# Second attention: the pattern of every second k replica added by a third matmul, evicted by ScalarE

## The chip, the cores and the metric

The kernel runs on one core of one Trainium2 chip, as one program in one launch. The core's engines are TensorE (PE), VectorE (DVE), ScalarE (ACT) and GpSimd (POOL), each with its own instruction queue, worked off in order; SyncE (SP) issues most of the transfers. The engines meet through semaphores. The metric is the device time of one execution in microseconds (us), lower is better.

## What is computed

The reference is a chain of four layers on 2048 tokens of width 128 (eight sequences of 256). Each layer is a mixer and a feed-forward part. The change touches the mixer of the third layer (in the kernel: the second attention, `l == 2`), an attention of 16 heads of width 8 with a relative position bias that depends on the distance only and is constant beyond the near keys:

```python
x = layernorm(h)
q, k, v = split_heads(x @ Wq), split_heads(x @ Wk), split_heads(x @ Wv)   # 8 x 16 heads x 256 x 8
scores = q @ k^T + bias[bucket(distance), head]
h = h + gate(softmax(scores) @ v @ Wo)
```

The second layer has an attention too (`l == 1`, without the bias). Both are made by the same functions.

## The kernel before, in words

Activations lie transposed in SBUF: 128 channels on the partitions, 2048 tokens along the free side, in four chunks (c = 0 to 3) of 512. A head has 8 channels, too few for a matmul's contraction, so each head gets a strip of 32 partitions, of which the last 24 hold three copies of its 8 channels (as high and low fp16 parts) and the first 8 helper rows. The helper rows of k serve to add constants to the scores: a row of ones (it meets the negated row maximum) and four rows that are 1 for far keys (they meet the far bias). This constant part of k is the tile `k_pat`, 128 partitions x 512, fp16. For the second attention GpSimd zeroes it (L1033) and twelve small transfers from `far_keys` put its rows in (`key_rows`, L2363 and L2366); the semaphore `k_rows` counts them. It stands at 64 after the first attention and at 256 (`16 * HH * 4`) once those of the second have landed.

Ahead of the main loop comes a preparation. A string, `PREPARE[l]`, writes down its units, and every engine goes through the same string and does its own part of each unit:
- D (D0 to D7): the dense product of a chunk with Wq or Wk on PE (L652). ACT makes the high fp16 part with the bias (`high`, L820), DVE the remainder (`low`, L937).
- R (R0 to R31): a replica. n even is q, n odd is k; four groups of heads for each of four chunks. PE adds up two matmuls, high part and low part, in a PSUM bank (L700, L701), and one engine evicts the bank to `q_st` or `k_st`. The q replicas are plain copies on ACT (L853). In the second attention DVE evicts all k replicas and adds `k_pat` in the same instruction (L981). In the first attention every second k replica is evicted by ACT with a per-partition bias, which works there since the pattern is the same for all keys. `by_act(l, m)` says who evicts, `evicted(A, m)` turns that into a semaphore and a count to wait for.
- WO, V: the output weights and the v projection, each with a bank of its own. R, WO and V share a ring of four banks: a unit waits until the one four places before it is evicted.
- F (F0 to F7): the first batch's scores (four L642 matmuls) into the one early pair of banks, and their row maxima on DVE (`row_maxima`: four custom instructions at L960). Each F on PE waits for the maxima of the F before it.
- X, N on ACT: fp16 copies of the normalised input (L832) and of the near bias table (L838), read by GpSimd later. B on DVE: the far bias rows and the conversion of the next layer's integer weights.

The main loop starts with S1.0 (again L642, for the next batch). It waits on PE for the last three evictions and for the maxima of F7. Each of its passes works on one batch: scores, row maxima on DVE, exponentials on ACT (L876), probabilities times v on PE (L806).

Nothing but the string and the semaphores sets the order. The wait for the rows stands once, on DVE, ahead of the whole preparation (L966).

Of the kernel before, what the change touches and what calls it, by code (L numbers as in the profile page):

```python
# [16 lines left out]
P = 128  # L17
# [17 lines left out]
HH = 4  # L35
# [52 lines left out]
def build(nc, x_in, pack0, packc, pack1, pack1f, pack2, far_keys, spread, onehot, wint, pack3, ew1, ew2, out):  # L88
    C0, N0 = columns(PACK0)
    with ExitStack() as ctx:  # L90
# [34 lines left out]
        ps = ctx.enter_context(nc.psum_tensor("ps", [P, 8, CH], F32))  # L125
# [357 lines left out]
        k_pat = take(CH // 2).bitcast(F16)  # L483
        rep_sel = take(4 * CH // 2).bitcast(F16).rearrange("p (x n) -> p x n", x=4)
        halves = [take(CH // 2).bitcast(F16) for _ in range(8)]
        hi_f, lo_f = halves[0:4], halves[4:8]
# [19 lines left out]
        ident16 = sb("ident16", [P, P], F16)  # L506
# [91 lines left out]
            return n if n < 4 else n % 2  # L598

        def by_act(l, m):  # L600
            return m % 2 == 0 or (l == 1 and m // 2 % 2 == 1)

        def evicted(A, m):
            l = 1 if A is ASEMS[0] else 2
# [17 lines left out]
        k_rows = sem("k_rows")  # L622
# [8 lines left out]
        def attn_pe(pe, l, A):  # L631
# [33 lines left out]
            for kind, n in PREPARE[l]:  # L665
                if kind in ("LG", "R", "WO", "V"):
                    bank = BANKS[l][(kind, n)]
                    r = IN_BANK[l].index((kind, n))
                    if r >= 4:
                        wait_bank(r - 4)  # L670
                if kind == "D":
                    dense(n)
                    if l == 2 and n == 3:
                        pe.wait_ge(rows_ready, 1)
                elif kind == "LG":
                    for t in range(4 * n, 4 * n + 4):
                        mm = pe.matmul(ps[:, bank, t % 4 * EXPERTS:(t % 4 + 1) * EXPERTS], xn[:, t * P:(t + 1) * P], WF("gate_w"),
                                       start=True, stop=True)
                    mm.then_inc(MOE["lg_ps"], 1)
                elif kind == "V":  # L680
                    for t in range(4 * n, 4 * n + 4):
                        mm = pe.matmul(ps[:, bank, (t % 4) * P:(t % 4 + 1) * P], xn[:, t * P:(t + 1) * P], WA(w, "Wv"),
                                       start=True, stop=True)
                    mm.then_inc(A["v_ps"], 1)
                elif kind == "WO":
                    pe.wait_ge(sel_done, 2)
                    pe.wait_ge(*A.at("v_zeroed", SEL_MADE))
                    for j in range(2):
                        pe.matmul(ps[:, bank, j * P:(j + 1) * P], ident, WA(w, "Wo")[:, 2 * j * P:(2 * j + 1) * P], start=True, stop=False)
                        pe.matmul(ps[:, bank, j * P:(j + 1) * P], shift16, WA(w, "Wo")[:, (2 * j + 1) * P:(2 * j + 2) * P], start=False, stop=True)  # L690
                    pe.matmul(ps[:, bank, 2 * P:2 * P + STRIP], shift16, WC("sel_sum"), start=True, stop=True).then_inc(A["wo_ps"], 1)
                elif kind == "R":
                    c, g, k = n // (2 * G4), n % (2 * G4) // 2, n % 2
                    d = 2 * c + k
                    if g == 0:
                        pe.wait_ge(*A.at("proj_lo", d + 1))
                    if n == 0:
                        pe.wait_ge(sel_done, 2)
                        pe.wait_ge(*A.at("v_zeroed", SEL_MADE))
                    pe.matmul(ps[:, bank, :], rep_sel[:, 2 * k, g * P:(g + 1) * P], hi_f[d % 4], start=True, stop=False)  # L700
                    pe.matmul(ps[:, bank, :], rep_sel[:, 2 * k + 1, g * P:(g + 1) * P], lo_f[d % 4], start=False, stop=True)\  # L701
                        .then_inc(A["rep_ps"], 1)
                elif kind == "F":
                    if n == 0:
                        pe.wait_ge(*A.at("proj_lo", 4))
                        for m in (2 * G4 - 3, 2 * G4 - 2, 2 * G4 - 1):
                            pe.wait_ge(*evicted(A, m))
                    else:
                        pe.wait_ge(*released(A, "S1", n - 1, -1))
                    scores(FIRST, n, -1)  # L710
# [101 lines left out]
        def attn_act(act, l, A):  # L812
# [11 lines left out]
            for kind, n in PREPARE[l]:  # L824
                if kind == "D":
                    high(n)
                    if l == 1 and n == 3:
                        act.wait_ge(k_rows, 16 * HH)
                        act.activation(k_ones, k_pat[:, 0:1], ACT.Copy).then_inc(A["rep_act"], 1)
                elif kind == "X":  # L830
                    xn_wait(act, 2)
                    act.activation(x16[:, n, 0, :], chunk(xn, n), ACT.Copy).then_inc(rows_ready, 1)  # L832
                elif kind == "N":
                    if n == 0:
                        act.wait_ge(tabs_in, 32)
                        act.wait_ge(S3["zeroed"], 16 * 7)
                    heads = slice(n * HEADS // 2, (n + 1) * HEADS // 2)
                    act.activation(near16[:, heads, :], near32[:, heads, ::-1], ACT.Copy).then_inc(near_high, 1)  # L838
                elif kind == "WO":
                    bank = BANKS[l][(kind, n)]  # L840
                    act.wait_ge(*A.at("wo_ps", 1))
                    act.activation(wo2.rearrange("p j n -> p (j n)"), ps[:, bank, 0:2 * P], ACT.Copy).then_inc(A["wo_done"], 1)
                    act.activation(by_group(sel_den)[:, :, 1, :], by_group(ps[:, bank, 2 * P:2 * P + STRIP])[:, :, 1, :], ACT.Copy).then_inc(A["wo_done"], 1)
                    act.activation(by_group(sel_den)[:, :, 0, :], by_group(WC("sel_sum"))[:, :, 0, :], ACT.Copy).then_inc(A["wo_done"], 1)
                elif kind == "R" and by_act(l, n):
                    c, g, k = n // (2 * G4), n % (2 * G4) // 2, n % 2
                    act.wait_ge(*A.at("rep_ps", n + 1))
                    to = (k_st if k else q_st)[:, g, c * CH:(c + 1) * CH]
                    if k:
                        act.wait_ge(*A.at("rep_act", 1))  # L850
                        act.activation(to, ps[:, BANKS[l][("R", n)], :], ACT.Identity, bias=k_ones).then_inc(A["rep_act"], 1)
                    else:
                        act.activation(to, ps[:, BANKS[l][("R", n)], :], ACT.Copy).then_inc(A["rep_act"], 1)  # L853
# [63 lines left out]
        def attn_dve(dve, l, A):  # L917
# [44 lines left out]
                                                       row_max[1 - par][:, qb, g, h:h + 1])  # L962
                        ins.then_inc(A["ttr"], 1)

            dve.wait_ge(k_rows, 16 * HH * (1 if l == 1 else 4))
            for kind, n in PREPARE[l]:  # L966
                if kind == "D":
                    low(n)
                elif kind == "LG":
                    dve.wait_ge(*MOE.at("lg_ps", n + 1))  # L970
                    dve.wait_ge(S3["zeroed"], 16 * 7)
                    dve.tensor_copy(rt["lg"][:, 4 * n:4 * n + 4, :],
                                    ps[:, BANKS[l][(kind, n)], 0:4 * EXPERTS].rearrange("p (t e) -> p t e", t=4)).then_inc(MOE["lg_sb"], 1)
                elif kind == "V":
                    dve.wait_ge(*A.at("v_ps", n + 1))
                    dve.tensor_tensor(v_sb[:, 4 * n:4 * n + 4, :].rearrange("p t c -> p (t c)"), ps[:, BANKS[l][(kind, n)], :], WA(w, "bv"),
                                      ALU.add).then_inc(A["v_done"], 1)
                elif kind == "R" and not by_act(l, n):
                    c, g = n // (2 * G4), n % (2 * G4) // 2
                    dve.wait_ge(*A.at("rep_ps", n + 1))  # L980
                    dve.tensor_tensor(k_st[:, g, c * CH:(c + 1) * CH], ps[:, BANKS[l][(kind, n)], :], k_pat, ALU.add).then_inc(A["rep_dve"], 1)  # L981
                elif kind == "F":
                    if l == 2 and n == 0:
                        dve.wait_ge(rows_out, 32)
                    row_maxima(n, -1)
                elif kind == "T":
                    if n < 3:
                        route1_choose(dve, n)
                    else:
                        route1_near(dve)  # L990
                elif kind == "B":
                    far_rows()
                    dve.wait_ge(w2_in, 16)
                    ups = 2 * HID2 * P
                    dve.tensor_scalar(w2f[:, ups:], wint_sb[:, ups:], 1.0 / (127.0 * W_DQ), None, ALU.mult)
                    dve.tensor_scalar(w2f[:, 0:ups], wint_sb[:, 0:ups], W_DQ / 127.0, None, ALU.mult).then_inc(w2_ready, 1)
# [1579 lines left out]
```

## Time and profile before

| | before |
|---|---|
| median of 3 runs | 835.33 us (833.63 to 836.16) |
| the profiled execution's own time | 835.67 us |
| its span | 833.9 us |
| PE busy | 702.1 us, 84% |
| DVE busy | 643.3 us, 77% |
| ACT busy | 507.6 us, 61% |
| GpSimd busy | 388.3 us, 47% |

The profiled execution took 1.8 us more than its span, the distance from the first to the last instruction in the trace. All points in time below count from the start of the span. The preparation of the second attention lies at 332 to 372 us, its main loop at 372 to about 500 us. The shares are means over the whole program; what a stage is worth has to be read in that stage.

### The profile page before, as it was taken

Reading aid. Unit: us, or ns where it says so; the run is one execution under the profiler, and the core shown is the slowest. Engines: PE = TensorE matmul, PEld = TensorE weight load, DVE = VectorE, ACT = ScalarE, POOL = GpSimd, SP = SyncE. Lnnn points to the kernel's source line nnn. Section 1 sums busy time; section 2 is a strip of 40 time slices with the busy share of each in tenths; the row PEclk is TensorE's granted clock in tenths of the full one; section 3 lists DMA queues with packets and bytes.
Section 4 is the critical chain, followed back from the end, with each engine's and each line's share of the span. In section 5 each row is a group of like instructions: output and inputs, shape, how many; then the busy total and the mean of one; then the engine's idle time right before and its main releaser. Section 6 shows DMA issues by size and latency. Waiting matters only on the chain.

```text
span 833.9 us, 13257 instructions
## 1 busy us (share of the span) xinstructions
PE 702.1 (84%) x4706; PEld 352.3 (42%) x4720; DVE 643.3 (77%) x1290; ACT 507.6 (61%) x746; POOL 388.3 (47%) x385
## 2 busy tenths in 40 slices
PE   5996987989979977869999989994877888888986
PEld 2332453444446753334444444441323344444453
DVE  3988777888727745787989924489899999899995
ACT  4788645888865545626666653668454555555473
POOL 0000305686836652041000002028999999999962
PEclk9996997999999996987999999997999999999999
DMA  8600000000144119100000000305447444645441
GB/s 348 277 1 0 4 1 1 1 31 23 37 117 132 44 28 298 42 0 2 3 2 3 2 2 1 126 16 166 159 154 276 147 149 143 201 162 178 156 161 51
DMA packets 30433, 75.97 MB, mean 91 GB/s; under 512 B 4335, under 2 KB 14008, under 8 KB 29344
## 3 DMA queue, kind: packets, MB, share of 16 engines
q1 hardware_dynamic: 26048, 67.41, 23.7%
q0 software_dynamic: 4320, 7.72, 2.7%
q8 instruction: 38, 0.62, 0.3%
q14 instruction: 27, 0.22, 0.1%
HBM read 59.28 MB, written 17.01 MB: 91 GB/s over the span
## 4 chain that ended last, share of the span: by engine, by line
PE 34%; DVE 22%; issue 18%; POOL 13%; ACT 10%; DMA 3%; SPq 0%; DVEq 0%; POOLq 0%; ACTq 0%
POOL arena L2231 7%; PE ps L806 4%; DVE ttr_out L960 4%; DVE xq L960 4%; DVE arena L2156 3%; DVE band L2163 3%; POOL exp_in L2198 3%; PE ps L784 2%; PE ps L642 2%; PE ps L295 2%; PE ps L1448 2%; ACT arena L876 2%; PE ps L652 1%; PE ps L772 1%; PE ps L1215 1%
## 5 line engine op out<-in xcount | busy, mean ns | idle before, releaser
L2156 DVE TENSOR_TENSOR_SCAN arena<-ps,arena 128x1024 f32<-128x1024 f32 x64 | 146.6, 2291 | 18.5 <-ACT ps L2032 9.8
L876 ACT ACTIVATE arena<-ps 128x1024 f32<-128x1024 f32 x128 | 124.8, 1025 | 35.3 <-PE ps L795 25.8
L2032 ACT ACTIVATE ps<-arena,negA 128x1024 f32<-128x1024 f32 x64 | 71.5, 1118 | 102.0 <-DVE arena L2156 101.7
L1866 PE MATMUL ps<-band,w 128*128 128x512 f32 x256 | 120.1, 592 | 0.0
L2163 DVE TENSOR_TENSOR band<-arena,ps 128x1024 f32<-128x1024 f32 x64 | 76.6, 1196 | 2.3 <-PE ps L1751 2.3
L2231 POOL TENSOR_TENSOR arena<-arena,gate 128x1024 f32<-128x1024 f32 x32 | 75.6, 2366 | 4.3 <-DMA gate<-b_dram 3.4
L2231 POOL TENSOR_TENSOR arena<-arena 128x1024 f32<-128x1024 f32 x32 | 75.2, 2364 | 0.3
L806 PE MATMUL ps<-arena 128*32 128x256 f32 x1024 | 70.9, 397 | 1.0 <-ACT arena L876 1.0
L1751 PE MATMUL ps<-xq,sel 128*128 128x512 bf16 x115 | 35.7, 383 | 41.8 <-DVE band L2163 39.1
L1074 POOL COPY arena<-arena 128x128 f32<-128x128 f32 x32 | 8.4, 296 | 123.7 <-PE ps L806 107.2
L1866 PEld LDWEIGHTS ps<-band,w 128*128 128x128 f32 x256 | 48.6, 190 | 40.2 <-issue 30.6
L784 PE MATMUL ps<-arena 32*128 32x256 f16 x512 | 49.9, 280 | 12.8 <-ACT arena L876 3.8
L2198 POOL DMA_INDIRECT exp_in<-wf,wa x32 | 32.2, 1007 | 57.3 <-DVE wa L2121 49.8
L642 PE MATMUL ps<-arena 32*128 32x256 f16 x512 | 50.2, 281 | 8.8 <-DVE arena L960 4.5
L1550 POOL DMA_INDIRECT e_out<-arena,band x39 | 37.9, 971 | 35.7 <-ACT arena L1499 21.7
L960 DVE CUSTOM_DVE_ANT_0 xq<-ps,wf 128x256 bf16<-128x256 f32 x128 | 46.5, 420 | 7.2 <-issue 7.2
L960 DVE CUSTOM_DVE_ANT_0 ttr_out<-ps,wf 128x256 bf16<-128x256 f32 x128 | 46.6, 420 | 6.8 <-issue 6.1
L947 DVE TENSOR_REDUCE xq<-ps 128x4 f16<-128x1024 f32 x32 | 38.4, 1222 | 11.1 <-PE ps L642 10.6
L947 DVE TENSOR_REDUCE arena<-ps 128x4 f16<-128x1024 f32 x32 | 38.7, 1220 | 7.1 <-PE ps L642 6.5
L1751 PEld LDWEIGHTS ps<-xq,sel 128*128 128x128 bf16 x128 | 8.0, 97 | 73.9 <-DVE band L2163 67.7
L806 PEld LDWEIGHTS ps<-arena 128*32 128x32 f32 x1024 | 27.4, 111 | 27.0 <-issue 12.5
L1381 POOL DMA_INDIRECT e_in<-arena,band x32 | 32.0, 1001 | 10.2 <-issue 8.5
(404 smaller groups left out, 1620.4 us busy)
## 6 DMA issues: line engine op xcount, KB each, us to landing
gate<-b_dram SPq DMA_DIRECT2D x32, 512.0 KB, 3.7
arena<-b_dram SPq DMA_DIRECT2D x32, 512.0 KB, 4.4
wf<-pack1f_dram SPq DMA_DIRECT2D x1, 3076.0 KB, 15.2
wf<-bias_rows SPq DMA_DIRECT2D x1, 3072.0 KB, 15.4
exp_in<-band SPq DMA_DIRECT2D x2, 1032.0 KB, 5.0
exp_out<-band SPq DMA_DIRECT2D x2, 1024.0 KB, 17.9
e_in<-band SPq DMA_DIRECT2D x2, 1024.0 KB, 21.7
arena<-e_out SPq DMA_DIRECT2D x4, 512.0 KB, 5.7
```

Of the source, the lines that this page charges most:

```text
L642: mm = pe.matmul(to[:, a:a + SEQ], q_st[h, g, (b + 1) * SEQ + qb * P:(b + 1) * SEQ + (qb + 1) * P], k_st[h, g, (b + 1) * SEQ:(b + 2) * SEQ ...
L784: mm = pe.matmul(out_[:, a:a + SEQ], k_st[h, g, b * SEQ + kb * P:b * SEQ + (kb + 1) * P], q_b[par][h, g, :], start=(l == 1 or kb == 0), st ...
L806: mm = pe.matmul(ps[32 * h:32 * h + 32, 6, (i // 2) * SEQ:(i // 2 + 1) * SEQ], v_b[pp][:, kb, i * HH + h, :], probs[i % 2][:, h, kb, :], s ...
L876: act.activation(probs[g % 2][:, 2 * pr:2 * pr + 2, :, :].rearrange("p h k n -> p (h k n)"), PAIRS[l][("S2", i, b)], ACT.Exp).then_inc(A[" ...
L947: dve.tensor_reduce(firsts.rearrange("p b h -> p h b"), scores.rearrange("p (h b n) -> p h b n", h=2, b=2), AX_X, ALU.max, negate=True).th ...
L960: ins = dve.tensor_tensor_reduce(ttr_outs[unit % 2][:, n, :], scores[:, n * SEQ:(n + 1) * SEQ], bias_q[:, g * HH + h, WIN - a - SEQ:WIN - ...
L1866: mm = pe.matmul(ps[:, j, :], ident, hc[i % 2][:, j * CH:(j + 1) * CH], start=False, stop=True, skip_group_check=True)
L2032: act.activation(dA_ps, dt3[:, cb, hf * HALF:(hf + 1) * HALF], ACT.Exp, scale=negA[:, cb * STATE + n:cb * STATE + n + 1]).then_inc(M["dA"], 1)
L2156: dve.tensor_tensor_scan(hst[i % 2], dA_ps, dbu[i % 4], 0.0, ALU.mult, ALU.add).then_inc(M["scan"], 1)
L2163: dve.tensor_tensor(hc[i % 2], hst[i % 2], pair(3), ALU.mult).then_inc(M["hc"], 1)
L2198: pool.indirect_dma_start(out=exp_in[k], out_offset=bass.IndirectOffsetOnAxis(ap=idx_s[:, k, t:t + 1], axis=0), in_=x_nat[:, t, :], in_off ...
L2231: pool.tensor_tensor(dbu[i % 4], du[:, cb, hf * HALF:(hf + 1) * HALF], b_sb[i % 4], ALU.mult).then_inc(M["dbu"], 1)
```

## The change

In the second attention, the k replicas n = 3, 7, 11, ..., 31 (eight of sixteen) get their pattern from a third matmul (`ident16` times `k_pat`) into the same bank, and ACT evicts them by a plain copy. The wait for all the rows moves from the head of DVE's preparation to the two places where the pattern is read: DVE's remaining eight additions, and the third matmuls on PE. What is left at the head asks for 64, which is there since the first attention. No function is new.

```diff
--- before.py
+++ after.py
@@ -598,7 +598,7 @@
             return n if n < 4 else n % 2
 
         def by_act(l, m):
-            return m % 2 == 0 or (l == 1 and m // 2 % 2 == 1)
+            return m % 2 == 0 or m // 2 % 2 == 1
 
         def evicted(A, m):
             l = 1 if A is ASEMS[0] else 2
@@ -698,8 +698,12 @@
                         pe.wait_ge(sel_done, 2)
                         pe.wait_ge(*A.at("v_zeroed", SEL_MADE))
                     pe.matmul(ps[:, bank, :], rep_sel[:, 2 * k, g * P:(g + 1) * P], hi_f[d % 4], start=True, stop=False)
-                    pe.matmul(ps[:, bank, :], rep_sel[:, 2 * k + 1, g * P:(g + 1) * P], lo_f[d % 4], start=False, stop=True)\
-                        .then_inc(A["rep_ps"], 1)
+                    patterned = l == 2 and k and by_act(l, n)
+                    mm = pe.matmul(ps[:, bank, :], rep_sel[:, 2 * k + 1, g * P:(g + 1) * P], lo_f[d % 4], start=False, stop=not patterned)
+                    if patterned:
+                        pe.wait_ge(k_rows, 16 * HH * 4)
+                        mm = pe.matmul(ps[:, bank, :], ident16[:, :], k_pat, start=False, stop=True)
+                    mm.then_inc(A["rep_ps"], 1)
                 elif kind == "F":
                     if n == 0:
                         pe.wait_ge(*A.at("proj_lo", 4))
@@ -846,7 +850,7 @@
                     c, g, k = n // (2 * G4), n % (2 * G4) // 2, n % 2
                     act.wait_ge(*A.at("rep_ps", n + 1))
                     to = (k_st if k else q_st)[:, g, c * CH:(c + 1) * CH]
-                    if k:
+                    if k and l == 1:
                         act.wait_ge(*A.at("rep_act", 1))
                         act.activation(to, ps[:, BANKS[l][("R", n)], :], ACT.Identity, bias=k_ones).then_inc(A["rep_act"], 1)
                     else:
@@ -962,7 +966,7 @@
                                                        row_max[1 - par][:, qb, g, h:h + 1])
                         ins.then_inc(A["ttr"], 1)
 
-            dve.wait_ge(k_rows, 16 * HH * (1 if l == 1 else 4))
+            dve.wait_ge(k_rows, 16 * HH)
             for kind, n in PREPARE[l]:
                 if kind == "D":
                     low(n)
@@ -978,6 +982,7 @@
                 elif kind == "R" and not by_act(l, n):
                     c, g = n // (2 * G4), n % (2 * G4) // 2
                     dve.wait_ge(*A.at("rep_ps", n + 1))
+                    dve.wait_ge(k_rows, 16 * HH * (1 if l == 1 else 4))
                     dve.tensor_tensor(k_st[:, g, c * CH:(c + 1) * CH], ps[:, BANKS[l][(kind, n)], :], k_pat, ALU.add).then_inc(A["rep_dve"], 1)
                 elif kind == "F":
                     if l == 2 and n == 0:
```

On DVE, at the head of the second attention's preparation, before (L242 ends the normalising, L937 are the low parts of D0 to D3, L981 the k evictions, `rep_ps` counts replicas on PE):

```order
L937 SCALAR_TENSOR_TENSOR arena<-ps,bq_s,arena 128x512 [waits attn_proj_hi,k_rows]
L937 SCALAR_TENSOR_TENSOR arena<-ps,wa,arena 128x512 [waits attn_proj_hi]
L937 SCALAR_TENSOR_TENSOR arena<-ps,bq_s,arena 128x512 [waits attn_proj_hi]
L937 SCALAR_TENSOR_TENSOR arena<-ps,wa,arena 128x512 [waits attn_proj_hi]
L981 TENSOR_TENSOR arena<-ps,arena 128x512 [waits attn_rep_ps] x6
L955 MEMSET wait_here 1x1 [waits attn_s1_ps,rows_out]
```

and now (L937 has become L941, L981 has become L986):

```order
L941 SCALAR_TENSOR_TENSOR arena<-ps,bq_s,arena 128x512 [waits attn_proj_hi,k_rows]
L941 SCALAR_TENSOR_TENSOR arena<-ps,wa,arena 128x512 [waits attn_proj_hi]
L941 SCALAR_TENSOR_TENSOR arena<-ps,bq_s,arena 128x512 [waits attn_proj_hi]
L941 SCALAR_TENSOR_TENSOR arena<-ps,wa,arena 128x512 [waits attn_proj_hi]
L986 TENSOR_TENSOR arena<-ps,arena 128x512 [waits k_rows,attn_rep_ps] x3
L959 MEMSET wait_here 1x1 [waits attn_s1_ps,rows_out]
```

Of the six k evictions between the low parts and F0, three are left, and each waits for the rows. (The first low part still names `k_rows`, with the count that is met.)

On DVE, at the end of the preparation, before (from the weight conversion of unit B on: R27, F6, R29, V3, F7, R31, and L1020 of the main loop; an F is one L955 and four pairs of L960):

```order
L996 TENSOR_SCALAR wint<-wint 128x768
L981 TENSOR_TENSOR arena<-ps,arena 128x512 [waits attn_rep_ps]
L955 MEMSET wait_here 1x1 [waits attn_ttr,attn_s1_ps]
L960 ISA ttr_out,arena<-ps,wf 128x256
...
L960 ISA arena 128x1
L981 TENSOR_TENSOR arena<-ps,arena 128x512 [waits attn_rep_ps]
L976 TENSOR_TENSOR arena<-ps,wa 128x512 [waits attn_v_ps]
L955 MEMSET wait_here 1x1 [waits attn_ttr,attn_s1_ps]
L960 ISA xq,arena<-ps,wf 128x256
...
L960 ISA arena 128x1
L981 TENSOR_TENSOR arena<-ps,arena 128x512 [waits attn_rep_ps]
L1020 TENSOR_SCALAR arena<-arena 128x32 [waits attn_ttr]
```

and now:

```order
L1001 TENSOR_SCALAR wint<-wint 128x768
L959 MEMSET wait_here 1x1 [waits attn_ttr,attn_s1_ps]
L964 ISA ttr_out,arena<-ps,wf 128x256
...
L964 ISA arena 128x1
L986 TENSOR_TENSOR arena<-ps,arena 128x512 [waits k_rows,attn_rep_ps]
L980 TENSOR_TENSOR arena<-ps,wa 128x512 [waits attn_v_ps]
L959 MEMSET wait_here 1x1 [waits attn_ttr,attn_s1_ps]
L964 ISA xq,arena<-ps,wf 128x256
...
L964 ISA arena 128x1
L1025 TENSOR_SCALAR arena<-arena 128x32 [waits attn_ttr]
```

R27 ahead of F6 and R31 behind F7 are gone.

On PE, from the dense products on, now (before, the row L705 isn't there, and L702 was L701; R0 to R3, then R4):

```order
L652 MATMUL ps<-xn,wa 128x512 [waits xn_ready,attn_bq_done]
L652 MATMUL ps<-xn,wa 128x512 [waits xn_ready] x3
L700 MATMUL ps<-arena 128x512 [waits sel_done,attn_v_zeroed,attn_proj_lo,rows_ready]
L702 MATMUL ps<-arena 128x512
L700 MATMUL ps<-arena 128x512 [waits attn_proj_lo]
L702 MATMUL ps<-arena 128x512
L700 MATMUL ps<-arena 128x512
L702 MATMUL ps<-arena 128x512
L700 MATMUL ps<-arena 128x512
L702 MATMUL ps<-arena 128x512
L705 MATMUL ps<-arena,ident 128x512 [waits k_rows]
L700 MATMUL ps<-arena 128x512 [waits attn_rep_act]
L702 MATMUL ps<-arena 128x512
```

The third matmul stands behind the two of R3, with a wait for the rows of its own.

## Rows read from the trace of the kernel before

**Rows 1.** Busy time by stretch: stretch, its length, busy us (instructions) by engine, clock, DMA.

```profile
345.00:360.00 15.00, 12.67 (x69) 6.07 (x66) 14.66 (x58) 10.19 (x17) 4.32 (x2) 1.00 0.01 1
```

**Rows 2.** Groups of instructions between 338 and 373 us: busy us, mean ns | idle before.

```profile
L853 ACT ACTIVATE arena<-ps 128x512 f16<-128x512 f32 x16 | 9.5, 596 | 14.9 <-PE ps L701 14.8
```

**Rows 3.** Who waited for whom, 338 to 373 us: us in total, times, longest.

```profile
ACT arena L853 <- PE ps L701: 14.8, 12, 4.7
...
DVE arena L937 <- DMA arena<-far_keys_dram: 2.9, 1, 2.9
```

**Rows 4.** Timeline of 332 to 341 us: start, length, engine, line [idle before <- releaser].

```profile
332.11 3.60 PE L652 MATMUL ps<-xn,wa 128*128 128x512 f32 x8
...
333.69 0.69 DVE L242 TENSOR_TENSOR xn<-arena,ps 128x512 f32<-128x512 f32 x1 [0.64 <-ACT arena L261]
...
335.74 0.69 ACT L820 ACTIVATE arena<-ps,wa 128x512 f16<-128x512 f32 x1 [0.17 <-PE ps L652]
337.28 0.75 DVE L937 SCALAR_TENSOR_TENSOR arena<-ps,bq_s,arena 128x512 f16<-128x512 f32 x1 [2.90 <-DMA arena<-far_keys_dram]
...
338.13 0.38 PE L700 MATMUL ps<-arena 128*128 128x512 f16 x1 [2.43 <-issue]
...
338.35 0.38 PE L701 MATMUL ps<-arena 128*128 128x512 f16 x1
...
339.92 1.28 DVE L981 TENSOR_TENSOR arena<-ps,arena 128x512 f16<-128x512 f32 x2
```

**Rows 5.** Timeline of 95.5 to 98 us, the same place in the first attention.

```profile
96.27 0.75 DVE L937 SCALAR_TENSOR_TENSOR arena<-ps,bq_s,arena 128x512 f16<-128x512 f32 x1
...
97.47 0.38 PE L700 MATMUL ps<-arena 128*128 128x512 f16 x1
```

**Rows 6.** Timeline of PE, 344 to 369 us: units F0, F2, F3, F4 and F7.

```profile
344.82 0.39 PE L642 MATMUL ps<-arena 32*128 32x256 f16 x4
...
350.85 0.39 PE L642 MATMUL ps<-arena 32*128 32x256 f16 x4 [0.77 <-DVE arena L960]
...
353.44 0.39 PE L642 MATMUL ps<-arena 32*128 32x256 f16 x4 [0.36 <-DVE arena L960]
...
356.02 0.39 PE L642 MATMUL ps<-arena 32*128 32x256 f16 x4 [0.34 <-DVE arena L960]
...
368.82 0.39 PE L642 MATMUL ps<-arena 32*128 32x256 f16 x4 [3.02 <-DVE arena L960]
```

**Rows 7.** Timeline of 366 to 373 us: R27, F6, R29 and R31 on DVE, S1.0 on PE.

```profile
366.69 0.69 DVE L981 TENSOR_TENSOR arena<-ps,arena 128x512 f16<-128x512 f32 x1
367.30 0.43 DVE L960 CUSTOM_DVE_ANT_0 ttr_out<-ps,wf 128x256 bf16<-128x256 f32 x1
...
368.68 0.69 DVE L981 TENSOR_TENSOR arena<-ps,arena 128x512 f16<-128x512 f32 x1
...
371.26 0.69 DVE L981 TENSOR_TENSOR arena<-ps,arena 128x512 f16<-128x512 f32 x1
...
372.17 0.61 PE L642 MATMUL ps<-arena 32*128 32x256 f16 x4 [1.98 <-DVE arena L981]
```

**Rows 8.** Busy time by stretch where the clock changes (columns as in rows 1).

```profile
131.50:132.00 0.50, 0.24 (x1) 0.27 (x2) 0.43 (x2) 0.50 (x3) 0.00 (x0) 0.75 0.00 0
370.50:371.00 0.50, 0.00 (x0) 0.00 (x0) 0.50 (x5) 0.00 (x0) 0.00 (x0) 0.69 0.00 0
384.00:384.50 0.50, 0.50 (x7) 0.13 (x4) 0.50 (x5) 0.26 (x1) 0.00 (x0) 0.66 0.00 0
```

**Rows 9.** Timeline of PE at the end of the first attention's preparation.

```profile
129.18 0.39 PE L642 MATMUL ps<-arena 32*128 32x256 f16 x4 [1.21 <-DVE arena L947]
...
131.76 0.55 PE L732 MATMUL ps<-band,w 128*128 128x129 f32 x1 [1.22 <-ACT arena L851]
```

**Rows 10.** Busy time by stretch: the main loop's start, and one later pass.

```profile
372.00:382.00 10.00, 9.18 (x78) 4.20 (x82) 5.87 (x37) 5.12 (x5) 0.00 (x0) 0.50 0.01 2
405.60:420.60 15.00, 14.73 (x207) 7.28 (x206) 13.56 (x78) 9.80 (x11) 0.53 (x2) 1.00 0.01 3
```

## The prediction

> **What bounds the kernel now.** I read the views in this order. First the busy time by stretch [rows 1]: between 345 and 360 us, inside the preparation of the second attention, DVE is busy 14.66 of 15 us and PE 12.67, while ACT has 10.19. DVE is the engine with no room here, PE comes next, ACT is third. Then the groups of that stage [rows 2]: ACT evicts its 16 q replicas at 596 ns each, while DVE's 16 k evictions take 0.69 us each [rows 7]. Then who waited for whom [rows 3]: ACT waited 14.8 us for PE in the same stage, and DVE waited once, 2.9 us, for the row transfers from far_keys. So the reader is to see two things: one long wait at the head of the stage, and a DVE queue which is late from there to the end.
>
> The head, in order of time [rows 4]: the last normalised chunk leaves DVE at 334.38, with the first high parts (L820) already made by ACT, and PE is done with the four dense products at 335.71 (332.11 + 3.60). But the first low part (L937) starts at 337.28, when the row transfers have landed, and the first replica matmul (R0) at 338.13, a hole of 2.43 us on PE. The low part doesn't read the pattern; it only stands behind the wait. In the first attention, where the transfers were there, the low part started at 96.27 and R0 at 97.47, 1.20 us later [rows 5].
>
> The rest: each F unit on PE (four L642 matmuls into the one early pair) waits for the row maxima of the F before it on DVE. The brackets on PE before F2, F3, F4 and F7 say 0.77, 0.36, 0.34 and 3.02 us [rows 6]. The stage ends when the first main-loop unit S1.0 starts, at 372.17, after 1.98 us of waiting for the last k eviction (R31), which DVE began at 371.26 [rows 7].
>
> **The change part by part.** I walk the queues from the head to S1.0 and write how far each point moves.
>
> *Rows awaited where needed.* low(0) can start when hi(0) is done and DVE is free of the normalising, about 334.4; R0 would be possible 1.20 us later, at 335.6, but PE itself is busy until 335.71. R0 moves from 338.13 to 335.75, by -2.4. The new waits: DVE waits for the rows at its first k eviction (R1), PE at the third matmul of R3. DVE comes to R1 after low(3), which needs ACT's hi(3) (335.74 + 0.69 = 336.43) and ends at about 337.2, so the landing at 337.28 costs DVE some 0.1 us. PE starts R3 at 335.75 + 3 x 0.44 = 337.1 and its third matmul at 337.5, after the landing. Behind PE's wait stand R4 and everything else of PE, and ACT's evictions behind those, but if the rows came later, the old order would be late by the same amount plus R0 to R3. The other row waits (DVE 8 evictions, PE 8 third matmuls) are always met; I take them at nothing.
>
> *The third matmul.* Successive f16 matmuls of 512 columns start 0.22 us apart, 338.13 and 338.35 [rows 4]. Eight are added: 1.8 us of PE. Bounds: nothing where PE waits for DVE anyway, 1.8 us where it is the bound.
>
> *The eviction.* Eight DVE evictions go. Each holds the next one up by 0.61 us, 366.69 to 367.30 [rows 7], together 4.9 us. ACT gets eight plain copies of 0.6 us, 4.8 us, against the 14.8 us in which it waits for PE in this stage [rows 3]. Bounds of the DVE gain: 4.9 if DVE set every piece, 0 if PE set all of them.
>
> Point by point:
> - R0 to F0 took 6.69 (338.13 to 344.82) [rows 4, 6]. PE sets it. Three third matmuls (R3, R7, R11) add 0.66. In return PE no longer meets the DVE backlog: before, DVE was in its low parts until 339.92, 1.8 us after R0, and each bank had to wait for it [rows 4]. Twelve pairs at 0.44 and the Wo unit of about 1.0 make 6.3, so 0.4 were such holes. Net +0.2: F0 moves by -2.2.
> - F0 to F2: the chain is dense product, high part, low part, F1 on DVE. R13 stays on DVE, R15 goes, but F2 only waits for F1. No gain: -2.2.
> - F2 to F3 took 2.59: on DVE F2 (1.38, as from 367.30 to 368.68 [rows 7]) and two evictions. Now R19 is gone and PE becomes the bound: 0.32 for F2, four pairs (1.75), one third matmul (0.22) = 2.29. Gain 0.3: -2.5.
> - F3 to F4 took 2.58, with 0.34 of waiting on PE [rows 6] plus the tail of the unit before, since the next matmul could start some 0.1 us before the modelled end. F3 now starts on DVE without a backlog, so this goes: -2.9.
> - F4 to F5: PE sends R22, R23, two dense products, and waits for their high and low parts. Same length: -2.9. F5 to F6: PE-bound, one third matmul: -2.7, but what counts next is DVE.
> - F6 to F7: DVE has F5, the V addition, the far rows and weight conversions, R27, F6; it is bound by itself, and R27 goes (0.61): F7 moves by -2.9 - 0.6 = -3.5.
> - F7 to S1.0: R31 goes from DVE, and S1.0 now waits for the maxima of F7, 0.6 earlier: **-4.1 at S1.0**.
>
> After S1.0 the order is the same, and nothing there waits on an absolute time: the rows, bias tables and conversions are ahead of it, and GpSimd's chain for S2.0 (from ACT's copies of xn) gets its input about 1.7 us earlier, as ACT's queue runs ahead. The whole shift of 4.1 us should reach the end. Against the profiled execution's own time of 835.67 this gives 831.6; the median of the runs shown is 0.34 lower, so 831.2.
>
> **The clock.** The granted clock fell from 1.00 to 0.50 at about 370.7, after a hole of 3.02, 1.4 us of matmuls, and the next hole; it came back at about 384.2 [rows 8]. In that time the first pass runs at 1.2 GHz with PE busy 9.18 of 10 us and DVE 5.87, where a later pass has DVE 13.56 of 15 [rows 10]. My walk leaves holes of 2.2 (before F7) and 1.2 us (before S1.0) with 1.5 us of matmuls between. In the first attention the holes were 1.21 and 1.22 us [rows 9], and the granted clock fell all the same, within the half us from 131.5 [rows 8]. So I keep the loss in the forecast.
>
> The Trainium skill, page "TensorE: Matmul & The Clock Gate", section "Why this matters for your kernels", says that it is long idle gaps between bursts of matmuls that bring the halved clock, and short ones don't. By that rule this change, which shortens the longest gap, could keep the full rate, and the time would be that of rival 1. The first attention's rows speak against it: the clock fell there after gaps of 1.2 us.
>
> **The rivals.**
> 1. *The clock stays up at the start of the main loop.* For it: the long hole shrinks from 3.02 to 2.2 us, and the hole of 2.43 us at the head did no harm. Against: the first attention. Price: from 372.2 to 384.2 PE runs at half rate, busy 0.92, which at most gives back 5.5 us; DVE idles 0.41 of it against 0.10 in a later pass, 3.7 us. I take 4: 827.2.
> 2. *Only the wait counts; the eviction gives nothing.* PE is 84% busy in the middle of the stage [rows 1], and the third matmuls take on PE what DVE gains. Then only -2.2 is left: 833.0.
> 3. *The change does nothing:* the row wait merely moves to R1 and R3 and PE is held by full banks behind R1 (ring of four) instead. For it: the landing time doesn't move. Against: R1 to R4 can be made meanwhile, and the low parts (2.6 us) are then done. 835.3.
> 4. *Slower: the clock stays down longer.* The half rate would have to reach into the second pass, where PE is busy 14.73 of 15 us [rows 10] and loses nearly half of each us. More than 4.1 + 2.5 us of loss needs over 13 us at half rate beyond the 12 of now; with half a pass more than that (20 us, 10 us of loss) the time is 841. For it: in the first attention the clock came and went twice. Against: in this one it came back and stayed.
>
> **How the numbers follow.** Forecast (around 4 us, 3 to 5.5) 0.53, rival 1 0.17, rival 2 0.16, rival 3 0.08, rival 4 0.06. No change can be told within 0.3%, 2.5 us. Faster: the forecast but for its edge, 0.50, rival 1, and a third of rival 2, since 2.2 is near 2.5: 0.72. Same: 0.03 + 0.11 + 0.08 = 0.22. Slower: 0.06. The range goes down to rival 1 and up past rival 2: 827.2 to 834.2.
>
> **What the profile after would show.** R0 at 335.7 with no wait for far_keys ahead of the low parts; F0 near 342.6, F4 near 353.1, F7 near 365.3, S1.0 near 368.1 and released by L960's successor, not by a k eviction; ACT with 24 replica copies in the stage and never the one that PE waits for; the clock at 0.50 from about 367. I would be wrong if a third matmul costs more than 0.22 us beside a weight load, if ACT's copies of xn and of the near tables delay an eviction on which a bank hangs, or if the clock does otherwise.

## The result, and the profile after

The changed kernel takes 832.46 us (median of 20 runs, 829.72 to 834.71) against 835.50 us for the kernel before (20 runs, 833.63 to 840.60). The ratio is 0.9959, 95% interval 0.9950 to 0.9969: 3 us faster, inside the forecast range, 1.3 us above the forecast time. Not all of it comes from the changed stage: 1.1 us arise at the very end of the program, as shown below. The profiled execution took 833.18 us with a span of 831.4.

Points in time of two executions are best compared from one mark just ahead of the stage, because the stages before it differ by up to 2.3 us from execution to execution (in one by 6 to 8). I take the start of the last L242, the last chunk of the normalised input on DVE: 333.69 us before, 334.63 after. From here on "at 35.42" means so many us behind this mark. The last column is ACT's first copy of the main loop, L863 in the kernel before and L867 in the changed one; it comes once per pass.

| us behind the mark | R0 | F0 | F2 | F4 | F7 | S1.0 | first L863/L867 |
|---|---|---|---|---|---|---|---|
| before | 4.44 | 11.13 | 17.16 | 22.33 | 35.13 | 38.48 | 40.94 |
| after | 1.86 | 8.81 | 14.84 | 19.40 | 32.57 | 35.42 | 37.89 |
| moved by | -2.58 | -2.32 | -2.32 | -2.93 | -2.56 | -3.06 | -3.05 |
| forecast | -2.4 | -2.2 | -2.2 | -2.9 | -3.5 | -4.1 | |

The head of the stage, timeline of the changed kernel on DVE and PE, answering to [rows 4]:

```profile
334.63 0.69 DVE L242 TENSOR_TENSOR xn<-arena,ps 128x512 f32<-128x512 f32 x1 [0.64 <-ACT arena L261]
335.28 0.75 DVE L941 SCALAR_TENSOR_TENSOR arena<-ps,bq_s,arena 128x512 f16<-128x512 f32 x1
...
336.49 0.38 PE L700 MATMUL ps<-arena 128*128 128x512 f16 x1
```

The low part follows the normalising without a pause, R0 comes 1.21 us later (1.20 in the first attention), and the wait for far_keys is gone from the row. The F units F3, F4 and F7 and the main loop's S1.0 on PE, answering to [rows 6] and [rows 7]:

```profile
351.84 0.39 PE L642 MATMUL ps<-arena 32*128 32x256 f16 x4
...
354.03 0.39 PE L642 MATMUL ps<-arena 32*128 32x256 f16 x4
...
367.20 0.39 PE L642 MATMUL ps<-arena 32*128 32x256 f16 x4 [2.96 <-DVE arena L964]
...
370.05 0.61 PE L642 MATMUL ps<-arena 32*128 32x256 f16 x4 [1.27 <-ACT arena L857]
```

The brackets of F3 and F4 have vanished: PE sets that part now. But the hole before F7 is 2.96 us, where it was 3.02. What DVE does in it is unit B, and its first row is not the one of before (DVE and POOL, timeline of the changed kernel):

```profile
362.20 1.04 DVE L926 COPY b_far<-wf 128x16 f32<-128x16 f32 x1
```

```profile
358.98 4.23 POOL L1067 TENSOR_TENSOR band<-arena,band 64x1024 f16<-64x1024 f32 x2
```

A copy of 128x16 elements takes 1.04 us and ends at 363.24, just as GpSimd's correction of the near table ends (363.21). In the kernel before the same copy started at 363.98, when GpSimd was nearly done (at 364.22), and took 0.28 us:

```profile
362.09 2.13 POOL L1062 TENSOR_TENSOR band<-arena,band 64x1024 f16<-64x1024 f32 x1
...
363.98 0.28 DVE L922 COPY b_far<-wf 128x16 f32<-128x16 f32 x1
```

By the busy time of the same 345 to 360 us [rows 1], which holds somewhat later work now, DVE went from 14.66 to 12.52 of 15 us and PE from 12.67 to 13.38.

The bracket before S1.0 names ACT's last eviction (L857), of R31. In this execution it ended at 369.42 and the maxima of F7 at 369.73, so that the maxima came last, as forecast. In the second execution (below) the clock fell while PE made R30 and R31: there the eviction ended at 369.76 and the maxima at 369.51, and PE did wait for ACT.

At the end of the program SyncE waits for the last transfer to `out_dram` (who waited for whom, the kernel before, then the kernel with the eviction alone):

```profile
SPq L90 <- DMA out_dram<-xT: 2.9, 1, 2.9
```

```profile
SPq L90 <- DMA out_dram<-xT: 1.8, 1, 1.8
```

From the end of DVE's last instruction to the landing of this transfer it takes 3.22 and 3.21 us in the two profiled executions of the kernel before, and 2.11 to 2.13 us in all twelve profiled executions of the other kernels, those of the changed one included. So 1.1 us of what each of them gains in time has nothing to do with S1.0. Why the transfer lands sooner stays open: no run changes it alone.

### The profile page after: what moved, and what is told of

Its sections match the earlier page's. It is cut to its first block, busy times and chain, and to the rows that moved or that the text cites. A ratio compares the mean times of both kernels' runs of the same rounds, so it can differ in the third digit from the quotient of the medians.

```text
span 831.4 us, 13289 instructions
## 1 busy us (share of the span) xinstructions
PE 705.7 (85%) x4714; PEld 354.2 (43%) x4728; DVE 639.7 (77%) x1282; ACT 511.7 (62%) x754; POOL 387.8 (47%) x385
## 4 chain that ended last, share of the span: by engine, by line
PE 36%; DVE 22%; issue 15%; POOL 12%; ACT 10%; DMA 3%; SPq 0%; DVEq 0%; POOLq 0%; ACTq 0%
POOL arena L2236 8%; PE ps L810 4%; DVE ttr_out L964 4%; DVE xq L964 4%; DVE arena L2161 3%; DVE band L2168 3%; PE ps L788 2%; PE ps L295 2%; PE ps L642 2%; PE ps L1453 2%; ACT arena L880 1%; PE ps L776 1%; PE ps L652 1%; POOL exp_in L2203 1%; PE ps L1220 1%
## 5 line engine op out<-in xcount | busy, mean ns | idle before, releaser
L857 ACT ACTIVATE arena<-ps 128x512 f16<-128x512 f32 x40 | 23.4, 595 | 23.2 <-PE ps L702 22.7
```

## The experiments

All but two were timed side by side with the kernel before (one was only profiled, one gave no result). "x" is the ratio to the kernel before with its 95% interval. The runs of one kernel spread by mostly 3 to 5 us, those of the kernel before by up to 9, so that the intervals are 0.002 to 0.0035 to each side. The profile, read from the mark, carries most of the verdicts. Each is one execution, though. Most pieces repeat to 0.1 us, but two things differ between executions of the same kernel: how late the rows land (it moves F0 by up to 0.6 us) and when the clock falls (it moves S1.0 by up to 0.6 us).

| | R0 | F0 | F7 | S1.0 | first L863/L867 | x |
|---|---|---|---|---|---|---|
| before, again | 4.63 | 11.32 | 35.34 | 38.68 | 41.15 | |
| wait only | 1.85 | 8.93 | 32.96 | 36.30 | 38.76 | 0.9941 (0.9920 to 0.9961) |
| eviction only | 4.05 | 11.20 | 34.97 | 38.66 | 41.12 | 0.9982 (0.9962 to 1.0002) |
| changed, again | 1.85 | 8.81 | 32.57 | 35.55 | 38.02 | 0.9939 (0.9913 to 0.9966) |
| changed, third | 1.85 | 9.06 | 32.81 | 36.29 | 38.76 | 0.9943 (0.9924 to 0.9962) |
| one matmul more | 1.85 | 9.46 | 33.44 | 37.05 | 39.51 | 0.9950 (0.9933 to 0.9966) |
| holes filled | 1.85 | 8.93 | 32.70 | 35.54 | 36.96 | 0.9940 (0.9920 to 0.9960) |
| GpSimd behind the far rows | 1.85 | 8.99 | 33.70 | 37.39 | 39.86 | 0.9962 (0.9942 to 0.9981) |
| GpSimd behind all of B | 1.85 | 8.81 | 31.55 | 34.40 | 36.86 | 0.9946 (0.9926 to 0.9966) |
| B ahead of F0 | 1.85 | 8.81 | 29.54 | 32.17 | 33.58 | 0.9900 (0.9865 to 0.9935) |
| wait only, B ahead of F0 | 1.86 | 8.34 | 31.61 | 34.95 | 37.42 | 0.9935 (0.9907 to 0.9963) |

**The wait alone.** The kernel before, with

```diff
-            dve.wait_ge(k_rows, 16 * HH * (1 if l == 1 else 4))
+            dve.wait_ge(k_rows, 16 * HH)
...
                     dve.wait_ge(*A.at("rep_ps", n + 1))
+                    dve.wait_ge(k_rows, 16 * HH * (1 if l == 1 else 4))
```

> The wait for the rows moved to where the pattern is read, every k replica still evicted by DVE. If the gain of the change is made of two parts that add (wait 2.3 to 2.6 us, eviction 0.5 to 1.6 us): S1.0 starts 2.4 to 2.6 us earlier after the last normalised chunk than before (35.9 us instead of 38.5), and the time is about 2.4 us under the kernel before (ratio 0.9971). If only the eviction counts and the wait is given back behind R1: no earlier S1.0, ratio 1.000.

S1.0 at 36.30, 2.18 us earlier than before; the time is 0.0059 down, 5 us by that interval's middle, where 2.4 was expected. The interval's upper end, 0.9961, is 3.3 us. Its own timeline on DVE and PE shows what is left of the wait:

```profile
336.81 2.08 DVE L982 TENSOR_TENSOR arena<-ps,arena 128x512 f16<-128x512 f32 x3 [0.50 <-DMA arena<-far_keys_dram]
...
337.55 0.39 PE L700 MATMUL ps<-arena 128*128 128x512 f16 x1 [0.60 <-DVE arena L982]
```

Half a us at R1, and PE feels it: R5 shares R1's bank and waits 0.60 us for its eviction. In the second execution of the same kernel the rows had landed before DVE came to R1; there F0 stands at 8.34 instead of 8.93, and S1.0 at 35.72 instead of 36.30. So the wait alone brings S1.0 2.2 to 2.8 us ahead of the first execution before, by how late the rows land.

**The eviction alone.** The changed kernel with the wait for all rows back at the head of DVE.

> The eight evictions moved to ACT with the third matmul, the wait for all rows left at the head of DVE. If the parts add: R0 as before, F0 0.4 us later than before (three more matmuls on PE), S1.0 about 1.3 us earlier by the walk, less 0.8 us if DVE's first copy of unit B meets GpSimd's long operation as it does in the changed kernel; ratio 0.9985 to 0.9995. If the eviction gives nothing: ratio 1.000 or, by 1.8 us of matmuls, 1.002.

From R0 to F7 it takes 30.92 us, before 30.69: nothing gained, where 0.5 us was expected at S1.0 with the longer copy in unit B. The copy took 1.05 us here too. That S1.0 is no earlier than before has to do with the clock, which fell here ahead of F7, so that the matmuls between F7 and S1.0 ran at half rate. The ratio allows anything from no gain to 3 us, and the 1.1 us of the last transfer are in it.

**Both again, side by side.**

> The changed kernel once more, on the same chip and in the same rounds as the wait alone with B moved. Ratio to the kernel before 0.995 to 0.997. The first pass of the main loop took 17.61 us with the clock back 13.2 us after the first L867, where the kernel before and the wait alone took 16.4 with the clock back after 8.4 to 9.7 us. If that belongs to the change: 17.6 us again. If it is chance from one execution to the next: either of the two.

> The wait alone, in the same rounds and on the same chip as the whole change. S1.0 again 36.3 us after the last normalised chunk. If the eviction's 0.8 us at S1.0 reach the end, this is 0.8 us above the changed kernel, ratio higher by 0.001; if the eviction costs later what it gains before S1.0, the two are equal or this one is faster.

> The whole change, in the same rounds as the wait alone. S1.0 again 35.4 to 35.6 us after the last normalised chunk, DVE's first copy of unit B again 1.04 us. Ratio 0.001 under the wait alone, if its 0.8 us reach the end.

Side by side the wait alone has 0.9939 (0.9920 to 0.9958) and the whole change 0.9943 (0.9924 to 0.9962): they can't be told apart. (The profiled execution of the second wait-only kernel had its mark 6 to 8 us later than the others; its F7 stands at 32.35, its first L863 at 38.18.) The second timing of the whole change, 0.9939, came out below the expected 0.995 to 0.997. Both expected places of S1.0 were missed. The wait alone has it at 35.72, not 36.3, since the rows came early. The third changed execution has it at 36.29, not 35.4 to 35.6: DVE waited 0.19 us for the rows (F0 at 9.06), and the clock fell 0.3 us behind F7, so that ACT's eviction of R31 was done 0.75 us behind F7's maxima. At the first L863/L867, where the eviction should have shown 1.6 us, the mean of two wait-only executions is 38.47 and of three changed ones 38.22. Where the rows came early and the clock fell late, S1.0 is at 35.72 with the wait alone and at 35.42 with the whole change. The wait carries the gain; the eviction adds some tenths of a us.

**One look at the kernel before.**

> The kernel before, profiled once more. S1.0 again 38.0 to 38.7 us after the last normalised chunk. The first pass again 16.5 us if its length belongs to the kernel, 16.5 or 17.6 if it is chance.

S1.0 stands at 38.68, as expected. The first pass took 17.61 us here. With the changed kernel's it makes a clear picture (ACT, timeline, the first two L867 of the changed kernel, first execution, then second):

```profile
372.52 1.02 ACT L867 ACTIVATE arena<-ps 128x1024 f16<-128x1024 f32 x1 [3.10 <-PE ps L754]
...
390.13 1.03 ACT L867 ACTIVATE arena<-ps 128x1024 f16<-128x1024 f32 x1 [1.63 <-PE ps L754]
```

```profile
372.43 1.02 ACT L867 ACTIVATE arena<-ps 128x1024 f16<-128x1024 f32 x1 [2.67 <-PE ps L754]
...
388.89 1.02 ACT L867 ACTIVATE arena<-ps 128x1024 f16<-128x1024 f32 x1 [1.75 <-PE ps L754]
```

17.61 and 16.46 us for the same kernel, as 16.47 and 17.61 for the kernel before and 16.40 and 17.62 for the wait alone. In the short ones the granted clock is back at 1.00 some 8 to 10 us after the first L867, in the long ones after 13 to 14 (in the changed kernel, 384 to 388 us, 0.78 in the first execution and 1.00 in the second). So the 1.14 us by which the first pass was longer in the first trace after are chance, not the change.

**One matmul more on PE.**

> The changed kernel with a fourth matmul in each of the eight patterned replicas: the high part is sent twice, the second one overwriting the first, so that the result is the same. It doubles what the third matmuls cost on PE. If my walk is right that PE sets R0 to F0 (three of the eight), F2 to F3 (one), and that F4 to F6 (two more) is PE-bound too, as the changed kernel's trace says: F0 0.65 us later, F7 and S1.0 1.1 to 1.4 us later than in the changed kernel (36.6 to 37.0 us after the last normalised chunk), time up by as much, ratio to the kernel before about 0.996. If DVE hides the matmuls: S1.0 within 0.3 us of 35.5, ratio 0.994 to 0.995.

In this form, with the group of the added matmul left open, the kernel gave no result. With a group of its own for the added matmul it ran:

```diff
+                    if l == 2 and k and by_act(l, n):
+                        pe.matmul(ps[:, bank, :], rep_sel[:, 2 * k, g * P:(g + 1) * P], hi_f[d % 4], start=True, stop=True)
                     pe.matmul(ps[:, bank, :], rep_sel[:, 2 * k, g * P:(g + 1) * P], hi_f[d % 4], start=True, stop=False)
```

> The changed kernel with a fourth matmul in each of the eight patterned replicas: the high part is sent twice, each a group of its own, the second overwriting the first, so that the result is the same. It doubles what the third matmuls cost on PE. If PE sets R0 to F0 (three of the eight), F2 to F3 (one) and F4 to F6 (two more): F0 0.65 us later, F7 and S1.0 1.1 to 1.4 us later than in the changed kernel (36.6 to 37.0 us after the last normalised chunk), ratio to the kernel before about 0.996. If DVE hides the matmuls: S1.0 within 0.3 us of 35.5, ratio 0.994 to 0.995.

F0 at 9.46 (+0.65), as expected, F7 at 33.44 (+0.87), where 1.1 to 1.4 was expected. Units F5 and F6 of this kernel (PE, timeline):

```profile
359.92 0.39 PE L642 MATMUL ps<-arena 32*128 32x256 f16 x4
...
362.62 0.39 PE L642 MATMUL ps<-arena 32*128 32x256 f16 x4
```

F4 to F5 takes 5.69 us, with the third matmul alone 5.47, without it 5.26; F5 to F6 2.70, 2.49, 2.27. So each added matmul lies on the path there with its full 0.21 us, and F5 is 1.08 us later than in the changed kernel, F6 1.29. F7 hangs on DVE, which comes from F5 and so reached unit B late enough to be held up 0.21 us less (the copy took 0.83 us): 1.08 - 0.21 = 0.87. S1.0 (37.05) isn't read: the clock fell 0.7 us behind F7.

**GpSimd's operation and unit B.** In the changed kernel, ahead of GpSimd's correction of the near table:

```diff
                 pool.wait_ge(*A.at("v_zeroed", ALL_ZEROED + 2))
+                pool.wait_ge(band_ready, 1)
```

> The changed kernel with one wait more: GpSimd begins its correction of the near table (4.2 us) only when DVE is done with the far rows of unit B. In the changed kernel DVE's first copy of B took 1.04 us instead of 0.28 and ended when GpSimd's operation did. If the copy was held up by GpSimd's operation: it takes 0.28 us again, F7 and S1.0 start 0.76 us earlier after the last normalised chunk (34.7 instead of 35.4), and S2.0 isn't delayed, since GpSimd ends at about 369.5. If the 1.04 us have another cause: no change in the copy. The time moves by 0.8 us at most, ratio to the kernel before 0.995 to 0.996.

The copy was short again, but the time was lost two instructions later (DVE, then POOL, of this kernel):

```profile
361.78 0.17 DVE L926 COPY b_far<-wf 128x16 f32<-128x16 f32 x1
...
363.78 2.51 DVE L1001 TENSOR_SCALAR wint<-wint 128x768 f32<-128x768 int32 x1
```

```profile
363.75 4.53 POOL L1068 TENSOR_TENSOR band<-arena,band 64x1024 f16<-64x1024 f32 x2 [5.25 <-issue]
```

S1.0 came 2 us late, not 0.8 early: 1.1 of them were lost at F7, the rest behind it, where the clock had fallen already. The wait had only moved the meeting onto the weight conversion. GpSimd lost too, 4.53 us where it took 4.23 before. With `w2_ready` in place of `band_ready`, which is set when B is all done:

> The changed kernel, GpSimd's correction of the near table now behind both the far rows and the weight conversions of unit B. Where it waited for the far rows alone, the copy took 0.17 us but the second conversion 2.51 instead of 0.56. If DVE's copies and conversions are held up whenever GpSimd's operation runs: the copy takes 0.17 to 0.28 us and the conversion 0.56, unit B takes 2.5 to 2.7 us instead of 3.5, F7 and S1.0 come 0.8 to 1.0 us earlier than in the changed kernel (34.5 to 34.7 us after the last normalised chunk). S2.0 may wait: GpSimd ends at about 369.5, S2.0 stands at 373 in the changed kernel, so it shouldn't. Ratio 0.993 to 0.996. If the long operations are slow for another reason, B takes 3.5 us again.

```profile
361.25 0.17 DVE L926 COPY b_far<-wf 128x16 f32<-128x16 f32 x1
...
363.23 0.56 DVE L1001 TENSOR_SCALAR wint<-wint 128x768 f32<-128x768 int32 x1
```

F7 at 31.55, S1.0 at 34.40, both 1.02 us earlier than in the changed kernel's first execution. Most of it is the copy, 0.17 instead of 1.04 us. In time it can't be told from the change (0.9946 and 0.9943, side by side).

**Unit B elsewhere.** The changed kernel with B moved in the string from behind V2 to ahead of F0 (and its wait for `rows_out` with it).

> The changed kernel with unit B (far bias rows and weight conversion, 3.5 us on DVE there) moved from between V2 and F6 to ahead of F0, where DVE idles 3.8 us. If DVE's work between F5 and F6 is what opens the 2.96 us hole on PE and eats the gain: the hole shrinks under 0.5 us, S1.0 starts 3 to 3.7 us earlier than in the changed kernel (31.7 to 32.4 us after the last normalised chunk instead of 35.4), ratio to the kernel before about 0.992. If moreover the clock stays at 1.00 because the hole is gone: ratio 0.988 to 0.989. If PE sets the end anyway: under 1 us, ratio 0.995.

F7 at 29.54 with no bracket, S1.0 at 32.17, 3.25 us earlier than in the changed kernel. F7 and the main-loop start (PE, timeline):

```profile
364.23 0.39 PE L642 MATMUL ps<-arena 32*128 32x256 f16 x4
...
366.86 0.39 PE L642 MATMUL ps<-arena 32*128 32x256 f16 x4 [1.05 <-ACT arena L857]
```

The clock stays at 1.00 past S1.0 here, until 371.8; the first pass takes 17.37 us all the same. The median is 828.06 us (6 runs), ratio 0.9900: the fastest kernel of the study. The same move in the kernel with the wait alone:

> The kernel with only the wait moved, and unit B ahead of F0 as in the run that gained 3.3 us at S1.0 over the changed kernel. Here DVE still evicts all k replicas. If the eviction on ACT is what makes room on DVE ahead of F0: B pushes F0 back by 2.5 us or more, and S1.0 comes at 35.7 to 36.2 us after the last normalised chunk, against 36.3 without the move; the eviction is then worth 3.5 to 4 us once B stands right. If DVE has room anyway: S1.0 at 33, and the eviction is worth nothing again. Ratio to the kernel before 0.993 to 0.994 in the first case, 0.990 in the second.

F1 on PE has to wait 1.63 us and F2 1.06, because DVE is full there; S1.0 at 34.95. F0 itself isn't pushed back (8.34). The rows came early here, as in the second wait-only execution, and against that one the move gains 0.77 us (35.72 to 34.95); with the eviction on ACT it gains 3.25 us. Put otherwise, the eviction is worth 0.3 us at S1.0 where B stands now (0.9 against the wait-only execution with late rows), and 2.8 us where B stands ahead of F0.

**The holes on PE filled.** The changed kernel with 13 matmuls (`ident16` times `k_pat` into the free bank 0) behind V3 and 5 behind R31.

> The changed kernel with 18 matmuls more that fill PE's two holes (13 behind V3, 5 behind R31) and whose result nobody reads. They cost at most 0.2 us at S1.0. If the holes make the clock fall: it stays at 1.00 through the first pass, which shortens from 17.6 us (first to second L867) to 13 to 14.5, and the time is 3 to 4 us under the changed kernel (ratio to the kernel before about 0.991). If the clock falls for another reason, or the first pass isn't bound by PE: same time as the changed kernel, ratio 0.996.

The holes are gone: 0.16 us before F7, 0.19 before S1.0. The clock holds past S1.0, and from 370 to 374 us PE is busy 3.35 of 4 us (PE, timeline, F7 and the place where the clock falls):

```profile
367.28 0.39 PE L642 MATMUL ps<-arena 32*128 32x256 f16 x4 [0.16 <-DVE arena L971]
...
374.86 0.60 PE L795 MATMUL ps<-arena 32*128 32x256 f16 x4 [0.66 <-DVE arena L971]
```

ACT's first copy comes 0.9 to 1.1 us earlier than in the first two changed executions, but then the clock falls in the main loop itself, at 374.8, behind gaps of 0.26, 0.23 and 0.66 us on PE, and is back only at about 385. The first pass takes 17.47 us, no less than without the fillers. In this execution the holes decided when the clock fell, not whether. So the 4 us of rival 1 were not to be had by closing the holes ahead of the main loop.

## Why the prediction came out as it did

- **R0, -2.4.** Right: -2.58 to the kernel's first execution, with R0 at 1.85 in every execution of a kernel that has the early low parts. The 0.2 are the modelled ends of matmuls: I let R0 wait until the dense products end (335.71), and it starts 0.16 us ahead of that (336.49 against 336.65 now).
- **R0 to F0, net +0.2.** Right: 6.95 instead of 6.69 us. The doubled matmul shows that PE sets it all. The share of the DVE backlog is right too: with the wait alone and early rows it takes 6.49 us.
- **F2 to F4.** Right: -0.6 us, the brackets gone.
- **F4 to F6: "Same length", and one third matmul.** Mis-sized by 0.2: R23's third matmul stands ahead of the dense product on PE and delays the chain of F5 too. F6 moved by 29.86 to 27.36, -2.50, where I had -2.7.
- **F6 to F7, "bound by itself, and R27 goes (0.61): F7 moves by -3.5".** This is the step that failed. F7 moved by -2.56. DVE's copy started 2.72 us earlier and GpSimd's correction only 1.96, so that the copy now fell 1.0 us ahead of the end of the second of GpSimd's two 2.1 us operations, and ended with it. Before, DVE reached that place 0.2 us ahead of the end. The sum comes out: -2.72 to the copy (0.2 less than the walk, by R23's matmul), 0.76 for the longer copy, -0.6 for R27. Both shifts stood in the prediction, 2.9 for DVE and 1.7 for GpSimd's input, but I had followed GpSimd's chain only for what waits for it by a semaphore. The run with GpSimd behind all of B gives the us back: -3.58 at F7.
- **F7 to S1.0, -0.6.** -0.50 in the first execution, where the clock fell late. Where it falls ahead of R30 and R31 the gain is lost again: the third changed execution has 3.48 us there, against 3.35 before. R31's third matmul and ACT's eviction behind it then come last, which the prediction excluded ("never the one that PE waits for"). The wait alone has 3.34 and 3.37 there.
- **The clock.** The loss was kept, as forecast, from 368.7 us instead of 367. The holes I expected (2.2 and 1.2 us) were 2.96 and 1.27. With gaps under 0.2 us ahead of the main loop, and none above 0.66 us in it, the clock fell all the same. The prediction cites the Trainium skill, page "TensorE: Matmul & The Clock Gate", section "Why this matters for your kernels", for long gaps as the cause; that run doesn't bear it out as the only one.
- **After S1.0, "the order is the same".** True of the order, but the last transfer lands 1.1 us sooner than in the kernel before, which the sum doesn't have.
- **Rivals.** Rival 2 was nearest to the truth in its mechanism (the wait carries the gain, and PE takes on part of what DVE gives), but its price (833.0, where 835.3 less 2.2 is 833.1) was too small a gain: the whole change saved 3.0, 5.1 and 4.8 us in its three timings, the wait alone 4.9 and 5.1 (3.3 to 6.7). Rivals 1, 3 and 4 did not happen.

That the time lay in the range is in part luck. Of the 4.1 us at S1.0 the walk gave 2.4 to the early R0 and the rest to the eviction, which brought some tenths; the last transfer made up for part of that.

The times of the wait alone (0.9941, 0.9939) lie lower than the 2.2 to 2.8 us at S1.0 explain. With the 1.1 us of the last transfer it is 3.3 to 3.9 us, at the lower end of the two intervals (3.3 to 6.7 and 3.5 to 6.7). The rest is within what executions differ by: from S1.0 to the end they take 458.5 to 462.6 us. Up to 1.4 us of that is the first pass. Another 1.5 us goes with the clock about 160 us behind the mark: it falls there for 6.8 us in most executions, but not at all in the first wait-only, the third changed and the doubled-matmul one, which are the shortest behind S1.0 (458.5 to 458.7). What decides it, and why the last transfer is slower in the kernel before, stays open.

## What to carry to other kernels

Move a wait to the instruction that needs the data before moving work between engines: two lines carried this gain, and the eight evictions added tenths of a us, since PE took on with the third matmuls a part of what DVE gave, and a longer copy in unit B took another. When an engine gets earlier relative to another, look at what both touch besides semaphores. And when load is taken off an engine, ask where the hole now is, and put a block there that can stand anywhere: the same eviction was worth 0.3 to 0.9 us at S1.0 before, and 2.8 us once unit B had moved into the slack that it opened. And when a gain in time is larger than the gain at the stage, look at the rest of the program, to its last transfer.

## What the runs showed of the hardware

GpSimd and DVE hold each other up without a semaphore. DVE's fp32 copy of 128x16 took 0.16 to 0.17 us with GpSimd idle, and 1.04 to 1.05 in five executions in which it began 1.0 us ahead of the end of a GpSimd operation, ending with it; a conversion of 128x768 took 2.51 instead of 0.56 when it met GpSimd's fp32 tensor_tensor. Evictions from PSUM beside the same GpSimd operation kept their 0.69 us. The Trainium skill says as much, page "GPSIMD Engine Reference", section "1. Specifications": the SBUF interfaces are shared with VectorE, with contention for DVE instructions in a mode of two ports or with two SBUF inputs. The rows agree in that the evictions, with one of their inputs in PSUM, kept their time; in which mode the copy and the conversion ran, no trace shows.

The granted clock came back in the first pass either 8 to 10 or 13 to 14 us after its first copy, by chance from one execution to the next of the same kernel, and the 3.7 to 5.2 us more at 1.2 GHz cost 1.14 to 1.22 us, some 0.2 to 0.3 us each. That price doesn't carry over: with the holes filled, only 10.2 us at 1.2 GHz, all inside the pass, still went with a pass of 17.47 us.

The last transfer to `out_dram` landed 3.2 us behind DVE's last instruction in both executions of the kernel before and 2.1 us behind it in the twelve others, with the same instructions at that place.
